# Routed expert layer: tokens sorted by expert in DRAM quarter by quarter, and the matmuls of 17 full slots placed around the convolution of the last quarter

## The chip, the cores and the metric

One Trainium2 chip (trn2), one core. The metric is the device time of one execution in microseconds (µs). The kernel before has a median of 687.84 µs over three runs (686.28, 688.94, 687.84).

## The reference, cut to what matters

The input has 8 sequences of 512 tokens with 1024 channels in float32, which are 4096 tokens in all. A depthwise causal convolution with 8 taps runs over each sequence, a router picks one of 8 experts for each convolved token, the token is multiplied by that expert's 1024 x 1024 matrix, and the original `x` is added.

```python
y = conv_general_dilated(x, cond_2048[:, None, :], window_strides=(1,), padding=[(7, 0)],
                         feature_group_count=1024) + L0_cond_b
idx = argmax(einsum('bsh,eh->bse', y, w_router), axis=-1)
all_out = einsum('bsh,efh->bsef', y, w_experts)
x = x + take_along_axis(all_out, idx[:, :, None, None], axis=2)[:, :, 0, :]
```

The inputs come from a fixed seed. For experts 0 to 7 the router's choices add up to 128, 227, 851, 1092, 528, 741, 367 and 162 tokens. In the first three quarters of the tokens they add up to 90, 173, 630, 839, 407, 527, 283 and 123.

## The kernel before, in words

The 1024 channels are 8 chunks (`HC`) of 128 partitions, and the 4096 tokens are four groups (a quarter each: two sequences, eight tiles of 128 tokens).

**Convolution.** For each group and chunk `x_sb` holds the channels as partitions and the tokens as columns. Of the 64 chunk-taps of a group TensorE takes 18, as matmuls by diagonal matrices (`conv()`, L525, two instructions for each of the two sequences), ScalarE takes one tap or the copy out of PSUM together with the bias (`seed()`, L277 and L282), and VectorE takes 42 as multiply-adds over 1024 columns (L359). TensorE then turns each finished chunk by transposes (`turn_y()`, L547) and interleaves the router's matmuls with them (`logits_of()`, L532). ScalarE copies the turned pieces out (`copy_out()`, L292), and SyncE stores them as rows of tokens in `y_dram` (`store_y()`).

**Routing, once, for all 32 tiles.** VectorE picks the expert of each token (L390 to L396), TensorE counts by two matmuls (L583, L584), and VectorE places each token (L402 to L422). One-hot matrices on VectorE and GpSimd and 32 small matmuls (L594) give the token of each row of each slot. A slot is 128 rows of one expert; each expert has its tokens rounded up to whole slots, 35 in all here.

**Slots.** Two slots are in flight (`RING`). For each slot GpSimd looks its indices up (L667), gathers 128 rows of `y_dram` (L682) and of `x` (L692), TensorE turns the rows back to channels by 8 transposes (`turn()`, L604), ScalarE writes the high part of a float32r pair (L323) and VectorE the rest (L478). TensorE does 48 matmuls of 512 columns (`gemm()`, L626: high by high, high by low, low by high), VectorE adds `x` (`residual()`, L472), and GpSimd scatters the 128 rows to `out` (L700). Where a slot begins another expert, ScalarE (`high()`, L298) and VectorE (`low()`, L365) split that expert's 8 weight chunks from `w_raw` into `w_sb`, each chunk once the slot ahead is through with it; SyncE refills `w_raw` behind them. There are seven such changes of expert.

TensorE alternates, by this order in `block.tensor`:

```python
turn(i, 1, False)
gemm(i, 0, False)
with pe.If(i < full):
    turn(i + 1, 0, False)
    gemm(i, 1, False)
```

## Time and profile before

| | |
|---|---|
| median of three runs | 687.84 µs (686.28 to 688.94) |
| the profiled execution: its time, its span | 687.4 µs, 685.6 µs |
| mean granted TensorE clock | 0.957 |
| TensorE (PE) busy | 635.6 µs, 93% |
| VectorE (DVE) busy | 382.0 µs, 56% |
| ScalarE (ACT) busy | 174.2 µs, 25% |
| GpSimd (POOL) busy | 157.1 µs, 23% |
| DMA | 118.13 MB, mean 172 GB/s |

The span runs from the first to the last instruction of the core. PE stands for TensorE's matmuls, PEld for its weight loads, POOLq and SPq for the queues on which GpSimd and SyncE issue DMAs. The granted clock is a share of 2.4 GHz: 1.00 is 2.4 GHz and 0.50 is 1.2 GHz. Matmul ends are modelled, so the spacing of many matmuls says more than the length of one.

### The profile page before, as it was taken

How to read it: one execution, taken by the hardware profiler on the slowest of the kernel's cores; microseconds unless marked ns; L12 is line 12 of the kernel's file. 1: busy time of each engine (PE TensorE's matmuls, PEld its weight loads, DVE VectorE, ACT ScalarE, POOL GpSimd, SP SyncE). 2: the span in 40 equal slices, each digit the busy share in tenths (PEclk: the TensorE clock that was granted, in tenths of full speed). 3: DMA queues.
4: the chain of work that ended last, by engine and by line, in shares of the span. 5: the costliest groups of instructions: out<-in, count | busy, mean ns of one | idle time of the engine just before them, and what ended most of it. 6: DMA issues, size and time to landing. Idle time of an engine off the chain costs nothing.

```text
span 685.6 us, 9583 instructions
## 1 busy us (share of the span) xinstructions
PE 635.6 (93%) x3058; PEld 488.1 (71%) x3059; DVE 382.0 (56%) x345; ACT 174.2 (25%) x199; POOL 157.1 (23%) x206
## 2 busy tenths in 40 slices
PE   1999999999999449999999999999999999999991
PEld 0556566666758338888888888888888888888881
DVE  5699999999999867531217212124411712181710
ACT  2124243323415215510106000014201500060600
POOL 5700000000000140233223332222323332222421
PEclk9989999999997559999999999999999999999996
DMA  8735275275321669574436743344743843476310
GB/s 291 290 124 161 84 246 165 86 238 182 107 78 62 214 206 371 195 287 148 142 122 218 258 144 124 126 135 148 294 144 104 317 156 127 128 277 220 96 65 8
DMA packets 50844, 118.13 MB, mean 172 GB/s; under 512 B 5520, under 2 KB 22032, under 8 KB 50832
## 3 DMA queue, kind: packets, MB, share of 16 engines
q1 hardware_dynamic: 35280, 67.64, 28.2%
q0 software_dynamic: 15552, 50.34, 21.9%
q8 instruction: 6, 0.10, 0.1%
q14 instruction: 6, 0.05, 0.0%
HBM read 89.13 MB, written 35.13 MB: 181 GB/s over the span
## 4 chain that ended last, share of the span: by engine, by line
PE 72%; issue 13%; DVE 9%; DMA 1%; POOL 1%; ACT 1%; SPq 0%; DVEq 0%; POOLq 0%; ACTq 0%
PE ps L626 56%; PE ps L525 8%; DVE y_t L359 6%; PE ps L604 5%; PE ps L547 2%; PE ps L532 1%; POOL diag L653 1%; DMA cst<-consts 1%; DVE x_sb L431 1%; DMA rows<-y_dram,idx 1%; DVE x_sb L428 0%; ACT y_t L277 0%; DVE x_sb L424 0%; DVE ys L478 0%; DVE rows L472 0%
## 5 line engine op out<-in xcount | busy, mean ns | idle before, releaser
L626 PE MATMUL ps<-w_sb,ys 128*128 128x512 f32 x1680 | 395.2, 394 | 0.0
L626 PEld LDWEIGHTS ps<-w_sb,ys 128*128 128x128 f32 x1680 | 314.1, 189 | 67.1
L359 DVE SCALAR_TENSOR_TENSOR y_t<-x_sb,taps,y_t 128x1024 f32<-128x1024 f32 x168 | 203.5, 1288 | 13.6 <-ACT y_t L282 7.0
L478 DVE TENSOR_TENSOR ys<-ps,ys 128x1024 fp32r<-128x1024 f32 x36 | 44.1, 1224 | 260.4 <-ACT ys L323 260.0
L525 PE MATMUL ps<-x_sb,diag 128*128 128x512 f32 x288 | 131.9, 613 | 13.9 <-POOL diag L653 13.9
L323 ACT CAST ys<-ps 128x1024 fp32r<-128x1024 f32 x36 | 36.5, 1014 | 317.6 <-PE ps L604 317.6
L525 PEld LDWEIGHTS ps<-x_sb,diag 128*128 128x128 f32 x288 | 55.1, 196 | 78.4 <-issue 78.4
L532 PEld LDWEIGHTS ps<-wr,y_t 128*128 128x128 f32 x512 | 76.4, 217 | 6.1 <-issue 4.3
L365 DVE TENSOR_TENSOR w_sb<-w_raw,w_sb 128x1024 fp32r<-128x1024 f32 x64 | 76.0, 1222 | 5.2 <-ACT w_sb L298 1.6
L532 PE MATMUL ps<-wr,y_t 128*128 128x8 f32 x512 | 75.6, 229 | 1.6 <-DVE y_t L359 1.6
L547 PE MATMUL ps<-cst,y_t 128*128 128x128 f32 x256 | 71.3, 316 | 0.8 <-ACT rows L292 0.8
L298 ACT CAST w_sb<-w_raw 128x1024 fp32r<-128x1024 f32 x64 | 66.5, 1050 | 19.4 <-PE ps L626 19.4
L700 POOL DMA_INDIRECT out<-rows,idx x35 | 36.2, 1034 | 118.1 <-DVE rows L472 101.0
L547 PEld LDWEIGHTS ps<-cst,y_t 128*128 128x128 f32 x256 | 54.6, 217 | 5.8 <-issue 4.2
L277 ACT ACTIVATE y_t<-ps,bias 128x1024 f32<-128x1024 f32 x16 | 17.9, 1116 | 127.1 <-PE ps L525 127.1
L662 POOL TENSOR_TENSOR x_sb<-x_sb,cst 128x1312 bf16<-128x1312 f32 x1 | 2.4, 2379 | 202.8 <-DVE x_sb L424 202.8
L604 PE MATMUL ps<-cst,rows 128*128 128x128 f32 x288 | 39.1, 281 | 9.8 <-DMA rows<-y_dram,idx 7.2
L667 POOL COPY idx<-ids_i 128x1 int32 (+1 forms) x73 | 18.1, 248 | 128.1 <-DMA out<-rows,idx 119.0
L472 DVE TENSOR_TENSOR rows<-ps,rows 128x1024 f32<-128x1024 f32 x35 | 42.5, 1216 | 7.6 <-PE ps L626 7.6
L692 POOL DMA_INDIRECT rows<-x_rows,idx x36 | 39.7, 1103 | 29.7 <-POOL idx L667 28.1
L682 POOL DMA_INDIRECT rows<-y_dram,idx x37 | 38.8, 1048 | 30.4 <-POOL idx L667 30.4
L604 PEld LDWEIGHTS ps<-cst,rows 128*128 128x128 f32 x288 | 34.9, 145 | 14.7 <-issue 7.4
(58 smaller groups left out, 107.5 us busy)
## 6 DMA issues: line engine op xcount, KB each, us to landing
w_raw<-experts SPq DMA_DIRECT2D x64, 512.0 KB, 6.0
x_sb<-x_t SPq DMA_DIRECT2D x32, 512.0 KB, 4.9
y_dram<-rows SPq DMA_DIRECT2D x16, 1024.0 KB, 5.6
rows<-y_dram,idx POOLq DMA_INDIRECT x37, 4.9
rows<-x_rows,idx POOLq DMA_INDIRECT x36, 4.4
out<-rows,idx POOLq DMA_INDIRECT x35, 3.4
cst<-consts SPq DMA_DIRECT2D x1, 377.0 KB, 9.1
cst<-consts SPq DMA_DIRECT2D x1, 64.0 KB, 5.1
```

The source lines that it names most:

```text
L298: nc.scalar.copy(w_sb[:, c * H:(c + 1) * H], w_raw[:, c % RAW, :]).then_inc(w_hi, 1)
L359: nc.vector.scalar_tensor_tensor(out=y, in0=x_sb[:, c, :, k:k + SEQ], scalar=taps[:, c, k:k + 1], in1=y, op0=ALU.mult, op1=ALU.add).then_i ...
L365: nc.vector.tensor_tensor(w_sb[:, (HC + c) * H:(HC + c + 1) * H], w_raw[:, c % RAW, :], w_sb[:, c * H:(c + 1) * H].bitcast(F32), ALU.subtr ...
L472: nc.vector.tensor_tensor(x_row[:, k, :], out_ps[k], x_row[:, k, :], ALU.add).then_inc(res_done, 1)
L478: nc.vector.tensor_tensor(ys[:, LO, k, :, :].rearrange("p c s -> p (c s)"), turn_both, ys[:, HI, k, :, :].rearrange("p c s -> p (c s)").bi ...
L525: mm = nc.tensor.matmul(conv_ps[n % 2][:, b, :], diag[:, DIAG[c, k], :], x_sb[:, c, b, k:k + SEQ], start=(k == PE_TAPS[c][0]), stop=(k == ...
L532: return nc.tensor.matmul(ps[:, 4, bass.ds((g * TPG + j) * EXPERTS, EXPERTS)], y_t[:, c, :, :].rearrange("p b s -> p (b s)")[:, j * P:(j + ...
L547: tr = nc.tensor.transpose(turn_ps[h][:, q * P:(q + 1) * P], y_t[:, c, :, :].rearrange("p b s -> p (b s)")[:, j * P:(j + 1) * P], ident)
L604: tr = nc.tensor.transpose(turn_ps[c // 4][:, c % 4 * P:(c % 4 + 1) * P], y_row[:, k, c * P:(c + 1) * P], ident)
L626: mm = nc.tensor.matmul(out_ps[k][:, f * HALF:(f + 1) * HALF], ys[:, a, k, c, :], w_sb[:, (b * HC + c) * H + f * HALF:(b * HC + c) * H + ( ...
L682: nc.gpsimd.indirect_dma_start(y_row[:, k, :], None, y_dram, at, bounds_check=last_token, oob_is_err=False).then_inc(y_got[k], 16)
L692: nc.gpsimd.indirect_dma_start(x_row[:, k, :], None, x_rows, at, bounds_check=last_token, oob_is_err=False).then_inc(x_got[k], 16)
```

## The change

The whole kernel is rearranged. The tokens are in the order of the input still, and the arithmetic of each token is the same.

- **Routing by quarter.** `choose(g)`, `rank(g)` and `place_rows(g)` run for each quarter of 8 tiles, on VectorE, TensorE and VectorE, among the taps of the quarter behind it. Each expert owns a region of 4096 rows in DRAM, and a running `base` for each expert says how far it is filled.
- **Sorting on the way out.** TensorE turns 8 chunks of one tile at a time (`turn()`), ScalarE copies the rows of 128 tokens out, and GpSimd scatters them straight to their sorted rows in `y_sorted` (`scatter_y()`), and their token numbers to `id_sorted` (`scatter_ids()`). The stores to `y_dram`, the one-hot matrices, their matmuls and the gathers of `y` are gone.
- **Two waves.** After three quarters `first_table()` lists 17 full slots (`FIRST_WAVE`). Their matmuls start then. VectorE does 4 taps of the last quarter in the gap and 4 behind each of the next slots; TensorE does that quarter's router matmuls, turns and counts behind slots 3, 4, 7, 11, 12 and 13 (`BEHIND`). `second_table()` runs on VectorE ahead of slot 15 and lists the remaining 18 slots.
- **Expert order.** Wave one takes the fullest expert first, which is expert 3, and then the others in order: 3 (6 slots), 1 (1), 2 (4), 4 (3), 5 (3). Wave two goes on with expert 5 (3 slots), then 0 (1), 1 (1), 2 (3), 3 (3), 4 (2), 6 (3), 7 (2). A change of expert falls on slots 6, 7, 11, 14, 20, 21, 22, 25, 28, 30 and 33 (counted from 0), which are eleven instead of seven.
- **Slots turned by VectorE.** ScalarE's queue loads 128 sorted rows by four DMAs of 32 partitions (`load_y()`), so laid out that a 32 x 32 block transpose on VectorE (`turn_blocks()`) gives the channels as partitions. The `experts` input is permuted to match. The token numbers come by a fifth DMA (`load_idx()`).
- **Last quarter.** It has 46 taps on VectorE and 13 on TensorE.

```diff
-PE_COUNT = [0, 0, 5, 4, 0, 0, 5, 4]
+EARLY = 3
+FIRST_WAVE = -(-(EARLY * TPG * P - EXPERTS * (P - 1)) // P)
+PE_COUNT = [[0, 0, 5, 4, 0, 0, 5, 4]] * EARLY + [[0, 0, 5, 5, 3, 0, 0, 0]] * (GROUPS - EARLY)
...
+        GAP_TAPS = (3, 1)
+        SLOT_TAPS = 4
+        BEHIND = {3: [("logits", 0), ("logits", 1)], 4: [("logits", 2), ("logits", 3)], 7: [("logits", 4), ("logits", 5)],
+                  11: [("logits", 6), ("logits", 7), ("turn", 0), ("turn", 1)],
+                  12: [("rank", 0), ("turn", 2), ("turn", 3), ("turn", 4)], 13: [("turn", 5), ("turn", 6), ("turn", 7)]}
+        CHOOSE_AT, PLACE_AT, TABLE_AT, SCATTER_AT = 12, 13, 14, 13
...
+            def load_y(w, n):
+                row = row_of(w, n)
+                src = y_sorted.rearrange("(r p) n -> r p n", p=P)[bass.ds(row, 1)].rearrange(
+                    "r (t i) (q f) -> (r i) q t f", t=4, q=4)
+                for q in range(4):
+                    nc.scalar.dma_start(y_blk[32 * q:32 * q + 32, :, :, :].rearrange("p t m f -> p t (m f)"),
+                                        src[:, q]).then_inc(y_got, 16)
...
+            for t in range(FIRST_WAVE):
+                w1, n1 = entry(t + 1)
+                w2, n2 = entry(t + 2)
+                high_y(t + 1, (t + 1) % RING, t + 1 < RING)
+                if (w2, n2) == (1, 0):
+                    sorted_is_out(1)
+                load_y(w2, n2)
...
+                load_idx(w1, n1, (t + 1) % IDX_RING, (t + 1 - IDX_RING) // RING + 1 if t + 1 >= IDX_RING else None)
+                high_w(w1, n1, t + 1)
...
+            for g in range(EARLY):
+                if g == 0:
+                    add_taps(PER_GROUP[0])
+                    continue
+                add_taps(5)
+                choose(g - 1)
+                add_taps(7)
+                place_rows(g - 1)
+                if g == EARLY - 1:
+                    find_first()
+                add_taps(PER_GROUP[g] - 12)
+            add_taps(GAP_TAPS[0])
+            choose(EARLY - 1)
+            add_taps(GAP_TAPS[1])
+            place_rows(EARLY - 1)
+            first_table()
...
+            for c in range(HC):
+                low(0, c)
+            turn_blocks(0, True)
+            low_y(0, 0)
+            for t in range(FIRST_WAVE):
...
+                if t == TABLE_AT:
+                    second_table()
+                turn_blocks(t + 1, False)
+                if t:
+                    residual(t - 1, (t - 1) % RING, (t - 1) // RING + 1)
+                low_y(t + 1, k)
+                add_taps(SLOT_TAPS)
+                low_w(w1, n1)
...
-            def turn(i, k, first):
-                pe.wait_ge(y_got[k], (i + 1) * 16)
...
-                    tr = nc.tensor.transpose(turn_ps[c // 4][:, c % 4 * P:(c % 4 + 1) * P],
-                                             y_row[:, k, c * P:(c + 1) * P], ident)
...
+            for t in range(FIRST_WAVE):
+                gemm(t, t % RING, *entry(t), t == 0)
+                for what, j in BEHIND.get(t, ()):
```

**TensorE, one slot of the loop, before.** `slot_expert` is the table of experts; L604 are the transposes.

```order
L602 ISA
L604 MATMUL ps<-cst,rows 128x128 x8
L610 ISA
L610 TENSOR_LOAD slot_expert
L610 ISA x2
L615 REGISTER_ALU
L622 ISA
L626 MATMUL ps<-w_sb,ys 128x512 x12
```

**TensorE, the end of a slot of wave one and the start of the next, in the change.** `tab_i` is the table, L782 are the router's matmuls for one chunk of the last quarter.

```order
L858 REGISTER_ALU
L862 MATMUL ps<-w_sb,ys 128x512 x12
L782 MATMUL ps<-wr,y_odd 128x8 x16
L846 TENSOR_LOAD tab_i
L846 ISA x2
L858 ISA
```

The eight transposes between two slots are gone, and behind four of the 35 slots such router matmuls stand in their place.

**VectorE, one slot, before.**

```order
L477 REGISTER_ALU
L478 TENSOR_TENSOR ys<-ps,ys 128x1024
L470 ISA
L472 TENSOR_TENSOR rows<-ps,rows 128x1024
L488 ISA
L488 TENSOR_LOAD slot_first
```

**VectorE, one slot of wave one, in the change.** L670 turns the blocks, L502 are taps of the last quarter.

```order
L670 STREAM_TRANSPOSE y_cols<-y_blk 128x4x8x32
L684 TENSOR_TENSOR x_row<-ps,x_row 128x1024
L675 TENSOR_TENSOR ys<-y_cols,ys 128x1024
L502 SCALAR_TENSOR_TENSOR y_odd<-x_own,taps,y_odd 128x1024 x4
L687 TENSOR_LOAD tab_i
L687 ISA x2
```

The transpose stands ahead of both, and four taps stand ahead of the weights of the next expert.

**ScalarE, one slot of wave one, in the change.** Before, L323 stood alone in this place.

```order
L384 DMA y_blk<-y_sorted 32x4x256
L377 TENSOR_LOAD tab_i
L377 ISA x2
L392 ISA
L392 DMA idx<-id_sorted 128x1
L406 TENSOR_LOAD tab_i
```

The first row is the last of four like it. ScalarE now issues five DMAs between writing `ys` and the weights.

## Rows read from the trace of the kernel before

**Rows 1.** Busy time by stage: us; PE, PEld, DVE, ACT, POOL busy; granted clock; DMA.

```profile
14.00:218.00 204.00, 201.94 (x1008) 128.86 (x1008) 197.40 (x164) 71.07 (x94) 15.96 (x15) 0.97 0.47 159
218.00:254.50 36.50, 16.95 (x98) 14.36 (x99) 28.64 (x49) 5.52 (x9) 9.05 (x11) 0.55 0.54 180
254.50:671.20 416.70, 416.61 (x1954) 344.73 (x1952) 148.54 (x127) 93.65 (x91) 125.16 (x171) 1.00 0.52 180
```

**Rows 2.** The chain that ended last, by engine, share of the span.

```profile
PE 72%; issue 13%; DVE 9%; DMA 1%; POOL 1%; ACT 1%; SPq 0%; DVEq 0%; POOLq 0%; ACTq 0%
```

**Rows 3.** The same chain in order of time: start, us, what; slots.

```profile
254.88 12.42 PE ps L626 x48
...
422.57 11.00 PE ps L626 x48
433.57 0.87 PE ps L604 x8
434.44 11.00 PE ps L626 x48
```

**Rows 4.** VectorE's taps (L359) alone, from 34 to 214 us.

```profile
34.00:214.00 180.00, 179.15 (x150) 0.98 0.45 146
```

**Rows 5.** TensorE and ScalarE in the convolution: chain, timeline, timeline.

```profile
51.63 6.97 PE ps L525 x16
...
209.16 3.86 PE L532 MATMUL ps<-wr,y_t 128*128 128x8 f32 x34
...
223.60 0.59 ACT L292 COPY rows<-ps 128x512 f32<-128x512 f32 x1 [0.27 <-PE ps L547]
```

**Rows 6.** Timeline of VectorE in the routing.

```profile
222.26 0.42 DVE L391 TENSOR_REDUCE top<-logits 128x32 f32<-128x256 f32 x1
...
226.28 0.69 DVE L402 TENSOR_TENSOR_SCAN scan<-cst,ps 128x256 f32<-128x256 f32 x1 [1.55 <-PE ps L584]
...
227.91 0.17 DVE L408 TENSOR_SCALAR small<-small 128x8 f32<-128x8 f32 x1
228.12 0.17 DVE L410 TENSOR_TENSOR_SCAN small<-cst,small 128x8 f32<-128x8 f32 x1
```

**Rows 7.** Groups of the page: line, engine, operation, count; busy, mean ns; idle before.

```profile
L478 DVE TENSOR_TENSOR ys<-ps,ys 128x1024 fp32r<-128x1024 f32 x36 | 44.1, 1224 | 260.4 <-ACT ys L323 260.0
L323 ACT CAST ys<-ps 128x1024 fp32r<-128x1024 f32 x36 | 36.5, 1014 | 317.6 <-PE ps L604 317.6
L365 DVE TENSOR_TENSOR w_sb<-w_raw,w_sb 128x1024 fp32r<-128x1024 f32 x64 | 76.0, 1222 | 5.2 <-ACT w_sb L298 1.6
L298 ACT CAST w_sb<-w_raw 128x1024 fp32r<-128x1024 f32 x64 | 66.5, 1050 | 19.4 <-PE ps L626 19.4
L472 DVE TENSOR_TENSOR rows<-ps,rows 128x1024 f32<-128x1024 f32 x35 | 42.5, 1216 | 7.6 <-PE ps L626 7.6
L700 POOL DMA_INDIRECT out<-rows,idx x35 | 36.2, 1034 | 118.1 <-DVE rows L472 101.0
```

**Rows 8.** Three DMA lines: issue ns min/median/max (x, weights); landing us of gathered rows (L682).

```profile
L219 SPq DMA_DIRECT2D x_sb<-x_t x32: 542/555/1199, 1.2 to 167.8; - x32
...
L227 SPq DMA_DIRECT2D w_raw<-experts x64: 332/333/997, 9.2 to 614.2; - x64
...
DMA to landing us min/median/max: 2.2/4.9/7.8
```

**Rows 9.** Granted clock around the end of the convolution (columns as in Rows 1).

```profile
209.00:213.00 4.00, 4.00 (x38) 3.92 (x36) 4.00 (x4) 3.65 (x5) 0.00 (x0) 1.00 0.54 180
213.00:214.00 1.00, 0.01 (x1) 0.00 (x0) 1.00 (x2) 1.00 (x2) 0.00 (x0) 0.72 0.96 322
214.00:222.00 8.00, 7.40 (x34) 7.31 (x35) 7.66 (x8) 3.51 (x4) 0.00 (x0) 0.50 0.01 3
```

**Rows 10.** Timeline: VectorE's first work behind the last tap; slot 0's matmuls.

```profile
218.04 3.49 DVE L365 TENSOR_TENSOR w_sb<-w_raw,w_sb 128x1024 fp32r<-128x1024 f32 x3
...
254.53 12.77 PE L626 MATMUL ps<-w_sb,ys 128*128 128x512 f32 x48
```

More of the change, by code:

```diff
@@ L330, in slot @@
                     for c in range(HC):
                         act.wait_ge(gemm_chunk, (t - 1) * HC + c + 1)
[L333 to L341 removed]
+                        high(nth, c)
@@ L489, in slot @@
                 with dve.If(new == 1):
[L490 removed]
+                    nth_load = dve.value_load(tab_i[0:1, w, 1, bass.ds(n, 1)], min_val=1, max_val=2 * EXPERTS - 1)
                     for c in range(HC):
[L492 to L497 removed]
```

1066 lines of the change are left out of this document (625 added, 441 removed).

## The prediction

> **What bounds the kernel now.** I read the stages first [rows 1]. They show three stretches. Up to 218 µs VectorE is busy for 197 of 204 µs and TensorE nearly as long. From 218 to 254.5 µs hardly anything is full, and the granted clock is 0.55. From there to 671 µs TensorE is full and VectorE has 148.5 µs of work in 416.7 µs. The chain that ended last agrees: TensorE has 72% of it [rows 2]. In order of time a slot is 48 matmuls in 11.00 µs and 8 transposes in 0.87 µs, so 11.87 µs, 35 times [rows 3]. In the first stage 150 taps took 179.15 µs, 1.194 µs each [rows 4], so a quarter of 42 taps is 50.1 µs. The last tap ends at 218.0 µs and slot 0 starts at 254.5 µs, a gap of 36.5 µs [rows 10]. The change works on all three stretches: it shortens the first by a quarter, keeps the gap, and takes the transposes off TensorE; in return the last quarter and four more changes of expert have to fit into the slots.
>
> **Term A, when slot 0 starts.** VectorE has three quarters of taps: 218.0 - 50.1 = 167.9 µs. Among them now stand two times choose() and place_rows() (11 operations each) and the 9 of find_first(). Operations on 8 columns are 0.21 µs apart (227.91 to 228.12) [rows 6]; 31 x 0.21 = 6.5, so 174.4. Beside it TensorE has in a quarter 72 conv instructions at 6.97/16 = 0.436 (31.4 µs), 128 router instructions at 3.86/34 = 0.114 (14.5 µs) [rows 5] and 64 turns at 0.87/8 = 0.109 (7.0 µs) [rows 3]. The turns no longer alternate with router work, so they wait for ScalarE: two halves take 0.44 + 0.27 + 0.59 = 1.30 µs [rows 5] and not 0.87, which is 8 x 0.43 = 3.4 µs. With 1.2 for the counts that is 57.5 µs, against 52.4 µs on VectorE. TensorE falls behind by 5 µs in each of the second and third quarters, of which find_first() gives back 2 and the three taps in the gap 3.6 of their own time; I take 5 µs of waiting ahead of choose(2). From there it is a sum: 174.4 + 3.6 (three taps) + 5 = 183.0; choose() 1.3; the counts 2.3 (two matmuls were waited for 1.55 [rows 6], nine here, one tap inside); place_rows() 1.1; first_table() and what precedes it, 38 operations, 12 of them on 152 to 256 columns at 0.36 (between 0.21 and 0.46, for which 256 columns give 0.42 busy [rows 6]) and 26 at 0.21, 9.8; the eight low() of the first expert at 3.49/3 = 1.16 [rows 10], 9.3. Then VectorE's turn of slot 0 (1.2, below), ScalarE's high part 1.0 [rows 7], its four DMA issues at 0.55 [rows 8] and the last seed 1.1, together 5.5 µs, behind which TensorE may start. The sum is 212.3, with 0.7 for handing over 213 µs. **Term A is 213 - 254.5 = -41.5 µs.** The other branch, turned rows through eight scatters (1.03 each to issue [rows 7]), landings and the load of slot 0, ends near 205 by the same rows and is covered by the eight low(); without them it would set the start.
>
> **Term B, the transposes.** 35 x 0.87 = **-30.5 µs**, since TensorE sets the pace of every slot. The load of the table entry now follows matmuls without transposes between; I cost it at nothing: the kernel before has the same load between transposes and matmuls, and they follow each other without a gap (433.57 + 0.87 = 434.44 [rows 3]). At worst the 0.87 had hidden it and comes back.
>
> **Term C, the last quarter's work on TensorE behind slots.** 14.5 router, 7.0 turns, 1.2 counts and some 3.0 of waits for ScalarE's copies: **+25.7 µs**. The 26 conv instructions of chunk 3 and 4 stay in the gap, under VectorE's table.
>
> **Term D, VectorE too late.** No row shows its transpose of 1024 float32 columns. The nearest rows are one-pass operations of the same size at 1.22 [rows 7]; below, half of that, above, twice. I take 1.2. The Trainium skill (VectorE: DVE Perf Modes, The three transpose paths) lists 311 ns for 128 columns of bf16; scaled by its own formula for the fixed part that is an estimate of about 1.25 µs, and no run here shows it. An iteration of wave one is then 3 x 1.22 + 4 x 1.19 = 8.4 µs and fits under 11.0. With a change of expert it is 8.4 + 8 x 1.2 = 18.0. Slots 6 and 7 change both: 36.0 against two slots and one slot of lead, 33.0, costs 3.0. The second table, 46 operations (11 long), is 11.5 µs. It stands behind the weights of slot 14, which end 2.3 µs into that slot (1.05 and 1.22 behind its predecessor's last chunk [rows 7]), and ahead of the turn, the residual and the low part of slot 15: 2.3 + 11.5 + 3.7 = 17.5 against 11.0 costs 6.5. In wave two ScalarE issues five DMAs, 2.8 µs, ahead of the first weights, so VectorE waits 2.4 and an iteration with a change is 3.7 + 2.4 + 9.6 = 15.7. Slots 20, 21 and 22 are 47.1 against 33.0 and a lead of 8: 6.1. Slots 28 and 30 lose 2.0. **Term D is +17.6 µs.** GpSimd loses the look-ups and one of three indirect DMAs per slot and is never last; SyncE's queue loses the stores, and its weights are asked for earlier.
>
> **Term E, the clock.** Slot 0 took 12.42 and not 11.00 µs behind the idle gap [rows 3]. I count four more such falls behind the waits above: **+5.6 µs**.
>
> **Sum.** -41.5 - 30.5 + 25.7 + 17.6 + 5.6 = -23.1, against the profiled execution's own 687.4 µs: **664.3 µs**. That execution lies 0.4 µs below the median of 687.84, so the two are the same here. The tail behind the last slot stays.
>
> **The rivals.**
> - *The ring of the y loads.* There is one `y_blk`. Each slot needs VectorE's turn 1.2, ScalarE's high part 1.0, four issues 2.2, and the landing L, one after the other: 4.4 + L. Above L = 6.6 µs this replaces 11.0 as the pace, and from there each change of expert costs its 4.7 in full, as no lead is left. Rows gathered from `y_dram` landed in 4.9 µs in the middle and 7.8 at most [rows 8]. For: four times 128 KB beside weights, with ScalarE issuing in the midst. Against: the median. At L = 7.0 it is 24 x 0.4 + 11 x 4.7 - 11.1 already counted = +50, less some 8 where term C overlaps: 706. It is the case of the other sign. Chance 0.13.
> - *TensorE slow in the first stage.* The granted clock fell to 0.50 behind a pause of 1.3 µs at 213 µs and stayed there for 8 µs, although TensorE was busy for 7.40 of them with router matmuls [rows 9]. Such stretches now stand in every quarter. The Trainium skill (TensorE: Matmul & The Clock Gate, Part 1) says that a sustained busy stretch releases the throttle; by it this rival would cost nothing, and the row speaks against relying on it. If half of the 21.5 µs of turns and router work and 3 µs of conv per quarter run at 0.50, two quarters lose 2 x (10.8 + 3) = 28, of which VectorE's slack covers some 12: 680. Chance 0.14.
> - *VectorE's transpose takes two passes.* 2.3 instead of 1.2 µs: 11 x 1.1 on the changes of expert and 8 of lead, +20: 684. Chance 0.10, split evenly between no change and slower.
> - *It goes better than I count.* Issues at 0.33 as for the weights [rows 8], no lag of TensorE, no falls of the clock: -5 - 6 - 4 = 649. Chance 0.15.
> - That it would not do what it says (the slots not starting before the last quarter) is excluded by the order of TensorE, which has slot 0 ahead of that quarter's router work.
>
> **How the numbers follow.** The forecast has 0.48, its own range 655 to 676. What a measurement can tell from no change is 0.5%, so 684.4 to 691.3. Faster: 0.48 + 0.14 + 0.15 = 0.77; same 0.05; slower 0.13 + 0.05 = 0.18. The range goes from the good case, 647, to where the ring has just begun to decide, 702.
>
> **What would show it.** First matmul of the slots at 213 µs (a later one: term A, and the wait ahead of choose(2) tells whether TensorE was behind). Slots without late work 11.0 µs apart (more: the ring, with VectorE waiting for `y_blk`). The transpose at 1.2 µs busy. Long slots at 3, 4, 7, 11 to 13 (term C), at 7, 15, 21 and 22 (term D). The prediction is wrong if the plain slots aren't near 11.0 or if slot 0 starts behind 225 µs.

## The result, and the profile after

The changed kernel took 754.52 µs (median of four executions, 742.73 to 755.06) against 687.06 for the kernel before beside it: a ratio of 1.087, 95% interval 1.076 to 1.098. Slower, where 664.3 was forecast, and 52 µs beyond the range. A second series gave 750.65 (six executions, 746.94 to 759.4, ratio 1.092, interval 1.088 to 1.097); single edits below are held against that one. The profiled execution is the shortest of all, 742.73 µs with a span of 740.9. The executions of 754 µs and more show a little less clock (0.89 to 0.90 against 0.91) and are not explained further than that, nor is one execution of e15 below, which took 938.09 µs at a mean clock of 0.64.

The page of the changed kernel: busy time, clock, DMA, and the engines' shares of the chain that ended last (TensorE had 72% there [rows 2]).

```profile
span 740.9 us, 9397 instructions
PE 640.8 (86%) x2752; PEld 483.2 (65%) x2753; DVE 476.8 (64%) x518; ACT 203.3 (27%) x231; POOL 202.6 (27%) x172
...
PEclk9997988799798599999999998699988999998997
...
DMA packets 67076, 139.90 MB, mean 189 GB/s; under 512 B 14304, under 2 KB 33760, under 8 KB 67040
...
PE 50%; DMA 14%; issue 10%; ACTq 8%; DVE 6%; ACT 6%; POOL 4%; DVEq 0%; SPq 0%; POOLq 0%
```

The same core by stretches (start and end, length, busy time and instructions of each engine, granted clock, DMA share, GB/s): the convolution up to the third `choose()`, the gap, slots 0 to 14, the crossing from one table to the other, and slots 17 to 34.

```profile
core 0: us, PE busy (x) PEld busy (x) DVE busy (x) ACT busy (x) POOL busy (x), PEclk, DMA share, GB/s
14.00:203.50 189.50, 186.14 (x767) 116.97 (x768) 156.71 (x156) 53.11 (x65) 62.06 (x52) 0.88 0.54 130
203.50:255.20 51.70, 23.81 (x107) 13.96 (x106) 24.23 (x62) 11.97 (x19) 19.22 (x16) 0.76 0.69 181
255.20:459.90 204.70, 194.67 (x922) 161.50 (x922) 153.11 (x176) 59.35 (x66) 54.06 (x44) 0.96 0.63 199
459.90:498.90 39.00, 27.84 (x96) 21.67 (x96) 7.16 (x6) 2.09 (x2) 12.17 (x13) 0.80 0.77 218
498.90:729.10 230.20, 208.09 (x864) 168.87 (x864) 128.06 (x110) 72.76 (x74) 46.99 (x38) 0.94 0.71 227
```

Held against [rows 1] and the forecast: slot 0 starts at 255.2, not at 213 (+42). Slots 0 to 14 with the last quarter behind them take 204.7 as against some 203 by the slots themselves with term C and the part of term D that falls there (+2). Slots 15 and 16 take 39.0, where two slots are 22 (+17). Slots 17 to 34 take 230.2; 18 slots at 11.0 and the forecast's 8 to 10 for changes of expert make 208 (+22). The tail gives 3 back. These make 80; the difference between 664.3 and 742.7 is 78, so they cover it within the rounding of the forecast's parts.

Where VectorE waited, from its timeline (start, length, engine, line, operation; in brackets the idle time ahead and what ended it):

```profile
139.83 0.23 DVE L527 TENSOR_REDUCE top<-ps 128x8 f32<-128x64 f32 x1 [9.94 <-PE ps L782]
203.54 0.22 DVE L527 TENSOR_REDUCE top<-ps 128x8 f32<-128x64 f32 x1 [8.01 <-PE ps L782]
218.57 9.17 DVE L660 TENSOR_TENSOR w_sb<-w_raw,w_sb 128x1024 fp32r<-128x1024 f32 x8
250.17 1.25 DVE L670 STREAM_TRANSPOSE y_cols<-y_blk 128x1024 f32<-128x1024 f32 x1 [22.43 <-DMA y_blk<-y_sorted]
...
301.64 1.22 DVE L684 TENSOR_TENSOR x_row<-ps,x_row 128x1024 f32<-128x1024 f32 x1 [2.58 <-PE ps L862]
...
475.29 1.25 DVE L670 STREAM_TRANSPOSE y_cols<-y_blk 128x1024 f32<-128x1024 f32 x1 [15.53 <-DMA y_blk<-y_sorted]
495.11 1.25 DVE L670 STREAM_TRANSPOSE y_cols<-y_blk 128x1024 f32<-128x1024 f32 x1 [16.25 <-DMA y_blk<-y_sorted]
...
530.90 9.17 DVE L660 TENSOR_TENSOR w_sb<-w_raw,w_sb 128x1024 fp32r<-128x1024 f32 x8 [5.30 <-ACT w_sb L368]
548.84 9.18 DVE L660 TENSOR_TENSOR w_sb<-w_raw,w_sb 128x1024 fp32r<-128x1024 f32 x8 [5.19 <-ACT w_sb L368]
```

The second and third `choose()` waited 9.9 and 8.0 µs for the router's matmuls (L782): TensorE, not VectorE, was last in the convolution. The eight `low()` ended at 227.7, and then VectorE waited 22.4 µs for the rows of slot 0. Plain slots are 10.9 µs apart, waiting for matmuls (L862), as forecast. The turns of slots 16 and 17, which follow the second table, waited 15.5 and 16.3 µs for rows. And at a change of expert VectorE waits over 5 µs for ScalarE's first high part (L368); the first three changes of the second wave, which follow each other directly, are 17.9 µs apart, where 15.7 was forecast.

TensorE ahead of the second and third `choose()`, where the router's matmuls of four chunks stand in one run of 64 instructions (L782), and the convolution's instructions (L768) behind the first and second such run:

```profile
73.21 8.72 PE L768 MATMUL ps<-x_own,diag 128*128 128x512 f32 x16
...
130.12 9.66 PE L782 MATMUL ps<-wr,y_odd 128*128 128x8 f32 x64
139.64 9.64 PE L768 MATMUL ps<-x_own,diag 128*128 128x512 f32 x16
...
192.75 10.75 PE L782 MATMUL ps<-wr,y_even 128*128 128x8 f32 x64
```

64 router instructions take 9.7 to 10.8 µs, where 64 times the 0.114 µs of [rows 5] is 7.3, and 16 conv instructions take 8.7 to 9.6 behind them instead of 6.97 [rows 5].

### The profile page after: what moved, and what is told of

Same layout as the page of the kernel before. It is cut to its first block, busy times and chain, and to the rows that moved or that the text cites. A ratio compares the mean times of both kernels' runs of the same rounds, so it can differ in the third digit from the quotient of the medians.

```text
span 740.9 us, 9397 instructions
## 1 busy us (share of the span) xinstructions
PE 640.8 (86%) x2752; PEld 483.2 (65%) x2753; DVE 476.8 (64%) x518; ACT 203.3 (27%) x231; POOL 202.6 (27%) x172
## 4 chain that ended last, share of the span: by engine, by line
PE 50%; DMA 14%; issue 10%; ACTq 8%; DVE 6%; ACT 6%; POOL 4%; DVEq 0%; SPq 0%; POOLq 0%
PE ps L862 23%; PE ps L768 16%; DMA y_blk<-y_sorted 9%; PE ps L782 9%; ACTq L384 4%; ACT w_sb L368 4%; DVE y_cols L670 3%; PE ps L804 3%; DVE w_sb L660 2%; DMA y_sorted<-row_own,fill_i 2%; ACTq L377 2%; POOL y_sorted L911 1%; POOL id_sorted L922 1%; DMA idx<-id_sorted 1%; POOL y_sorted L931 1%
## 5 line engine op out<-in xcount | busy, mean ns | idle before, releaser
L862 PE MATMUL ps<-w_sb,ys 128*128 128x512 f32 x1680 | 407.2, 405 | 66.8 <-ACT y_odd L342 26.8
L862 PEld LDWEIGHTS ps<-w_sb,ys 128*128 128x128 f32 x1680 | 329.3, 197 | 143.5 <-DVE w_sb L660 27.8
L670 DVE STREAM_TRANSPOSE y_cols<-y_blk 128x1024 f32<-128x1024 f32 x36 | 44.7, 1241 | 123.2 <-DMA y_blk<-y_sorted 123.2
L942 POOL DMA_INDIRECT x_row<-x_rows,idx x36 | 43.1, 1198 | 253.5 <-DMA idx<-id_sorted 212.3
L368 ACT CAST w_sb<-w_raw 128x1024 fp32r<-128x1024 f32 x96 | 93.4, 1045 | 60.1 <-PE ps L862 32.1
L502 DVE SCALAR_TENSOR_TENSOR y_odd<-x_own,taps,y_odd 128x1024 f32<-128x1024 f32 x74 | 90.8, 1279 | 4.8 <-ACT y_odd L346 4.6
L768 PE MATMUL ps<-x_own,diag 128*128 128x512 f32 x160 | 79.7, 658 | 13.8 <-POOL diag L897 13.8
L502 DVE SCALAR_TENSOR_TENSOR y_even<-x_own,taps,y_even 128x1024 f32<-128x1024 f32 x56 | 70.3, 1303 | 15.7 <-ACT y_even L346 6.9
L950 POOL DMA_INDIRECT out<-x_row,idx x35 | 45.0, 1286 | 121.1 <-DVE x_row L684 115.8
L768 PEld LDWEIGHTS ps<-x_own,diag 128*128 128x128 f32 x160 | 33.4, 214 | 53.6 <-issue 53.6
L684 DVE TENSOR_TENSOR x_row<-ps,x_row 128x1024 f32<-128x1024 f32 x35 | 41.7, 1191 | 22.4 <-PE ps L862 22.4
L768 PE MATMUL ps<-x_ext,diag 128*128 128x512 f32 x108 | 52.5, 641 | 0.0
L675 DVE TENSOR_TENSOR ys<-y_cols,ys 128x1024 fp32r<-128x1024 f32 x36 | 44.1, 1226 | 6.2 <-ACT ys L401 4.5
L922 POOL DMA_INDIRECT id_sorted<-token,pos_i x32 | 41.7, 1304 | 9.8 <-issue 9.8
L782 PEld LDWEIGHTS ps<-wr,y_even 128*128 128x128 f32 x256 | 36.4, 229 | 2.9 <-issue 2.4
L768 PEld LDWEIGHTS ps<-x_ext,diag 128*128 128x128 f32 x108 | 21.6, 206 | 25.5 <-issue 25.5
L782 PE MATMUL ps<-wr,y_even 128*128 128x8 f32 x256 | 35.8, 282 | 0.0
L502 DVE SCALAR_TENSOR_TENSOR y_even<-x_ext,taps,y_even 128x1024 f32<-128x1024 f32 x28 | 34.8, 1278 | 0.1
L782 PEld LDWEIGHTS ps<-wr,y_odd 128*128 128x128 f32 x256 | 33.2, 211 | 1.8 <-issue 1.4
```

Of the source, the lines that this page charges most:

```text
L368: nc.scalar.copy(w_sb[:, c * H:(c + 1) * H], w_raw[:, c, :]).then_inc(w_hi, 1)
L502: nc.vector.scalar_tensor_tensor(out=y, in0=x_tile(g, c)[:, :, k:k + SEQ], scalar=taps[:, c, k:k + 1], in1=y, op0=ALU.mult, op1=ALU.add).t ...
L670: nc.vector.transpose(y_cols[:, :, :].rearrange("p m (t i) -> p t m i", t=4), y_blk[:, :, :, :]).then_inc(y_blocks, 1)
L675: nc.vector.tensor_tensor(ys[:, LO, k, :, :].rearrange("p c s -> p (c s)"), y_cols[:, :, :].rearrange("p c s -> p (c s)"), ys[:, HI, k, :, ...
L684: nc.vector.tensor_tensor(x_row[:, k, :], out_ps[k], x_row[:, k, :], ALU.add).then_inc(res_done, 1)
L768: mm = nc.tensor.matmul(conv_ps[n % 2][:, b, :], diag[:, DIAG[c, k], :], x_tile(g, c)[:, b, k:k + SEQ], start=(k == 0), stop=(k == PE_COUN ...
```

## The experiments

Four causes were on the table. **Theory 1**: the 32 scatters of 4-byte ids clog the DMA engines. **Theory 2**: TensorE's clock falls behind the long router runs and makes it last in the convolution. **Theory 3**: the 4 MB of the second expert's weights, asked for at 220 µs, hold up the rows of slot 0. **Theory 4**: what ScalarE issues ahead of the first high part stretches a change of expert. Each was first edited without the others; e1 leaves out the eight late fills too, the scatters by which GpSimd pads each expert's last block of 128 rows.

| run | edit | µs | ratio to before (95%) |
|---|---|---|---|
| e11 | none, the changed kernel again | 750.65 | 1.0922 (1.0879 to 1.0965) |
| e1 | no id scatters, no late fills | 729.89 | 1.0604 (1.0547 to 1.0662) |
| e2 | second expert's weights behind slot 0's rows | 741.43 | 1.0777 (1.0751 to 1.0803) |
| e3 | one conv unit moved within the router's run | 752.6 | 1.0954 (1.0889 to 1.1019) |
| e4 | ids asked for by GpSimd | 737.6 | 1.0716 (1.0689 to 1.0743) |
| e5 | router matmuls between conv matmuls | 738.87 | 1.0753 (1.0711 to 1.0795) |
| e6 | two conv taps fewer on TensorE | 740.71 | 1.0754 (1.0694 to 1.0813) |
| e7 | second table behind the slot's work | 751.39 | 1.0947 (1.0897 to 1.0996) |
| e16 | ids of 32 bytes | 728.07 | 1.0568 (1.0537 to 1.0598) |
| e13 | two row buffers | 724.96 | 1.0541 (1.0516 to 1.0566) |
| e14 | turns back in the second wave | 754.07 | 1.0967 (1.0924 to 1.101) |
| e8 | e4 and ids in the rows | 711.63 | 1.0378 (1.0319 to 1.0438) |
| e10 | e9 with id scatters | 721.49 | 1.0495 (1.0465 to 1.0525) |
| e9 | all mends | 687.44 | 1.0004 (0.9982 to 1.0026) |
| e12 | e9 and two row buffers | 672.95 | 0.9768 (0.9743 to 0.9794) |
| e15 | e12, turns back in the second wave | 683.93 | 0.9926 (0.9904 to 0.9949) |

### Theory 1: scatters of 4 bytes (e1, e8, e16)

```diff
 for g in range(EARLY):
     scatter_y(g)
-    scatter_ids(g)
+# id_sorted is written once at the start from a constant list (e1)
```

> The 32 scatters of 4-byte token ids and the 8 late scatters that fill the last blocks are left out. The ids come from a constant table (a fixed list of all tokens, with the real number per expert), written to id_sorted at the start; the rest rows are copied there at the start too, so the later gathers, scatters and loads move as many bytes as before. The rows that leave are therefore paired with other tokens' x. Theory 1 (these tiny transfers clog the DMA engines and hold up the loads of sorted rows): the last tap of the third quarter moves from 191.9 to about 187, slot 0 starts at 245 instead of 255.2 (landing of its rows 7 us instead of 13.8), the two waits of 15.5 and 16.3 us at slots 16 and 17 shrink to under 3 us together with the second table's, total about 716 against 742.7. Rival (weights asked for at the same moment, theory 3, and ScalarE's issues, theory 4, hold the rows up): slot 0 at 253, wait at slot 16 still 10 us, total 735.

e1 pairs rows with the wrong tokens' `x`, so it is no version of the layer and only its time counts. It took 729.89, 21 µs less than the changed kernel. The rows of slot 0 were there 36.0 µs behind the third `choose()` instead of 46.6, as theory 1 had it, and the residual of slot 16 came 65 µs behind that of slot 12, not 81. The start of the slots gained less than that, since this execution's third `choose()` came at 210.4, with a 12.6 µs wait for TensorE. But the forecast of 716 was missed, and 735 was the rival's: slots 16 and 17 still waited 9.4 and 8.6 µs for rows, not under 3. So the scatters (with the fills) cost 21 µs here, and of the waits that remain, 11.0 µs at slot 0 and these two, they are not the cause.

e8 keeps the result whole and carries the id in the row:

```diff
-y_sorted = nc.dram_tensor("y_sorted", [EXPERTS * TOKENS, H], F32, ...)
+y_sorted = nc.dram_tensor("y_sorted", [EXPERTS * TOKENS, H + 8], F32, ...)
+nc.gpsimd.tensor_copy(row_buf(g, j)[0][:, H:].bitcast(I32), token[:, n:n + 1].to_broadcast([P, 8]))
```

> The token's id travels in eight added columns of each sorted row (1032 columns), written by GpSimd ahead of the scatter; the 32 scatters of 4-byte ids are gone, and nothing of the result changes. It has the ids loaded by GpSimd as in the run before, so it is held against that run's 737.6 us. Theory 1 (4-byte scatters clog the DMA engines): rows of slot 0 land 8 to 10 us earlier behind the third choose, residual of slot 14 to that of slot 17 falls from 76 us to 62, total 714. Rival (bytes and issues, not their size): within 5 us of 737.6, or above it, since rows of 4128 bytes are more bytes and GpSimd has 32 copies more.

711.63 against e4's 737.6: 26 µs, as theory 1 has it. VectorE's wait for slot 0 fell to 12.3, slot 16's residual came 66 µs behind slot 12's instead of e4's 76 (the expectations of e7 and e8 name slots 14 and 17 for this stretch, but their 81 and 76 are the times from slot 12 to 16), and from `choose()` to the rows it is 36.3 µs:

```profile
203.34 0.23 DVE L507 TENSOR_REDUCE top<-ps 128x8 f32<-128x64 f32 x1 [8.39 <-PE ps L762]
...
239.61 1.25 DVE L650 STREAM_TRANSPOSE y_cols<-y_blk 128x1024 f32<-128x1024 f32 x1 [12.26 <-DMA y_blk<-y_sorted]
```

e16 asks what about the scatters does it, with as many of them and elements of 32 bytes:

```diff
-id_sorted = nc.dram_tensor("id_sorted", [EXPERTS * TOKENS, 1], I32, ...)
+id_sorted = nc.dram_tensor("id_sorted", [EXPERTS * TOKENS, 8], I32, ...)
```

> The changed kernel with every id repeated eight times in its sorted row, so that the 32 id scatters move elements of 32 bytes instead of 4, as many of them as before; the initial fill of the id table is 1 MB instead of 128 KB. If the element's size of 4 bytes is what clogs the DMA engines, most of theory 1's gain comes without carrying the ids in the rows: rows of slot 0 land 36 to 38 us behind the third choose instead of 46.6, residual of slot 12 to that of slot 16 falls from 81 to 66 us, total 725 to 730. If the number of tiny elements does it (128 per scatter, whatever their size), everything stays: 745 to 755.

728.07: as much as e1 gained. The rows came 36.9 µs behind `choose()`, slot 16's residual 71 µs behind slot 12's. So between these two it is the size of 4 bytes and not the number of elements; sizes between 4 and 32 bytes were not tried. ScalarE asked for the rows of slot 0 at the same time in both, at 230.6 and 231.6 µs, but its four issues took 9.0 µs in the changed kernel and 1.9 in e16. At the crossing e16 parts the two waits. Slot 16's falls from 15.5 to 2.6 µs, slot 17's does not:

```profile
457.26 1.25 DVE L670 STREAM_TRANSPOSE y_cols<-y_blk 128x1024 f32<-128x1024 f32 x1 [2.61 <-DMA y_blk<-y_sorted]
482.06 1.25 DVE L670 STREAM_TRANSPOSE y_cols<-y_blk 128x1024 f32<-128x1024 f32 x1 [21.16 <-DMA y_blk<-y_sorted]
```

The DMA view of one stretch, 116 to 136 µs, in which SyncE loads `x` for the next quarter: first the changed kernel, then e16. Both issue the eight id scatters of the first quarter from about 101 to 115 µs; their last 32 packets are recorded inside the stretch in the changed kernel and ahead of it in e16. In these views q0 is GpSimd's queue, q1 SyncE's and q10 ScalarE's.

```profile
DMA packets 554, 1.02 MB, mean 51 GB/s; under 512 B 55, under 2 KB 55, under 8 KB 554
...
q1 hardware_dynamic: 522, 1.02, 90.2%
q0 software_dynamic: 32, 0.00, 0.1%
...
x_ext<-x_t SPq DMA_DIRECT2D x2, 512.0 KB, 17.8
```

```profile
DMA packets 1089, 2.11 MB, mean 106 GB/s; under 512 B 64, under 2 KB 64, under 8 KB 1088
...
q1 hardware_dynamic: 1088, 2.10, 33.1%
...
x_ext<-x_t SPq DMA_DIRECT2D x3, 512.0 KB, 3.6
```

The id packets themselves are 32 in 20 µs and take 0.1% of the engines' time, so a list by queue clears them. The harm is in the other queue: 522 packets of 2 KB hold the engines for 90% of 16 x 20 µs, 0.55 µs each, while e16's take 0.10, and a load of 512 KB lands in 17.8 µs instead of 3.6. It is the same from 451 to 461 µs, where both kernels issue id scatters and ScalarE's queue (q10) brings the rows of slot 16. In the changed kernel 10 of its packets hold 45% of 16 x 10 µs, in e16 720 hold 17%:

```profile
q10 hardware_dynamic: 10, 0.01, 45.2%
```

```profile
q10 hardware_dynamic: 720, 0.53, 17.3%
```

What inside an engine holds these packets up, no trace shows.

### Theory 3 and theory 4 (e2, e4)

```diff
 sp.wait_ge(table_ready, w + 1)
+if w == 0:
+    sp.wait_ge(y_got, 64)
```

> SyncE asks for the second expert's weights only when the rows of slot 0 have landed. Theory 3 (the 4 MB burst holds those rows up): their last landing falls from 13.8 us to 7, slot 0 starts at 248 and the total is 736. Theory 1 (the id scatters do): landing stays at 11 to 13 us, slot 0 at 253, total 741. Either way slot 3 or so may wait for weights by up to 3 us if the delay is too long.

741.43, 9 µs less by the medians, though its profile ends level with the changed kernel's shortest execution. The wait for slot 0's rows fell from 22.4 to 13.7, so the burst does hold them up; but slot 1's then waited 9.8 behind it, and of the 8 µs it was ahead at slot 3 it had lost 3 by slot 6, where the first changes of expert wait for these weights. The burst was moved more than removed. Theories 1 and 3 share these rows: the burst and the scatters are in flight together, and what each takes alone can't be added.

```diff
-load_idx(1, n + 1, r, ...)            # ScalarE
+load_idx(1, n + 3, (m + 3) % IDX_RING)  # GpSimd, a slot ahead
```

> The 36 loads of a slot's ids leave ScalarE's queue and are issued by GpSimd, one slot ahead. Theory 4 (in the second wave ScalarE's issues and table reads ahead of the first high part make a change of expert 18.0 us): VectorE's wait for it falls from 4.9 to 3.2 us, consecutive changes stand 16.3 apart, some 9 changes give 12 us, total 731. Rival (it is DMA traffic): changes stay 17.5 to 18.0 apart, total 741 to 745, and the later issues on GpSimd's queue cost up to 5.

737.6. The wait for ScalarE's first high part fell from over 5 µs to about 3, and the changes stand 15.9 and 15.6 µs apart, which is what the prediction had counted, though with five issues on ScalarE, where four are left here:

```profile
531.58 9.17 DVE L644 TENSOR_TENSOR w_sb<-w_raw,w_sb 128x1024 fp32r<-128x1024 f32 x8 [2.64 <-ACT w_sb L368]
...
547.45 9.18 DVE L644 TENSOR_TENSOR w_sb<-w_raw,w_sb 128x1024 fp32r<-128x1024 f32 x8 [3.10 <-ACT w_sb L368]
...
563.09 8.04 DVE L644 TENSOR_TENSOR w_sb<-w_raw,w_sb 128x1024 fp32r<-128x1024 f32 x7 [2.90 <-ACT w_sb L368]
```

Theory 4 stands. Of the queue's order `load_y()`, `load_idx()`, `high_w()`, the one small load with its table read was worth 2.1 µs per change. The 731 expected was set against the short execution of 742.7; against 750.65 the gain is the 12 to 13 µs forecast.

### Theory 2: TensorE in the convolution (e3, e5, e6)

```diff
-conv(g + 1, 2)
 for c in range(4, 6):
     logits(g, c)
+conv(g + 1, 2)
```

> In every quarter the conv of chunk 2 of the next quarter stands between the router work of chunks 4, 5 and that of 6, 7, so that no 32 router matmuls follow each other. Theory 2 (TensorE's granted clock falls behind the long run of router matmuls and makes TensorE the bound of the convolution): granted clock at 0.50 only for half as long between 60 and 200 us, the wait ahead of the third choose falls from 8.0 to 3 us, slot 0 starts at 250, total 737. Rival (the fall comes from router matmuls in any grouping, or TensorE is simply too full): waits unchanged within 1.5 us, total 742 to 745, as the conv that VectorE needs comes later.

752.6: nothing gained. But the edit does not do what its expectation says. Each chunk is 16 router instructions. In the changed kernel they stand in runs of 32, 32 and 64, and moving the conv behind chunks 4 and 5 makes runs of 32, 64 and 32: the run of 64 is moved, not cut. TensorE's timeline in the first quarter, from chunks 2 and 3 on, has the 64 parted only by a wait of 1.75 µs for VectorE:

```profile
50.40 3.63 PE L782 MATMUL ps<-wr,y_even 128*128 128x8 f32 x32
55.78 7.00 PE L782 MATMUL ps<-wr,y_even 128*128 128x8 f32 x32 [1.75 <-DVE y_even L502]
62.63 10.45 PE L768 MATMUL ps<-x_own,diag 128*128 128x512 f32 x20
72.92 3.89 PE L782 MATMUL ps<-wr,y_even 128*128 128x8 f32 x32
76.66 8.54 PE L768 MATMUL ps<-x_own,diag 128*128 128x512 f32 x16
```

Behind the 64 router instructions 20 conv instructions took 10.45 µs, where 20 x 0.436 is 8.7, and behind the 32 the 16 took 8.54, where 6.97 is their time at full clock. The mean clock from 73 to 139.8 µs is 0.82, where the changed kernel has 0.83. So e3 says nothing for or against shorter runs. e5 spreads the router matmuls, some four to eight instructions behind every two of the convolution:

```diff
-for c in range(2): logits(g, c)
-conv(g, 7)
-for c in range(2, 4): logits(g, c)
-conv(g + 1, 2)
-for c in range(4, 6): logits(g, c)
+mixed([conv_parts(g, 7)], [logit_parts(g, c) for c in (0, 1)])
+mixed([conv_parts(g + 1, 2)], [logit_parts(g, c) for c in range(2, 6)])
```

> The router matmuls of chunks 0 to 5 stand one by one between the conv matmuls of chunk 7 and of the next quarter's chunk 2 (two or three behind each), so that at most 32 router instructions follow each other, as in the kernel before. Theory 2a (long runs of 8-column matmuls make the granted clock fall): mean clock of 73 to 203 us 0.95 instead of 0.85, third choose at 196 instead of 203.5, slot 0 at 248, total 736. Theory 2b (the clock falls in the turns, with their waits for ScalarE's copies, or by itself): clock and choose as before within 2 us, total 740 to 745.

738.87, 12 µs less. Between 73 and 139.8 µs the granted clock is 0.97, where the changed kernel had 0.83 with as busy a TensorE (64.45 and 65.29 of 66.80 µs). In the kernel before, whose clock was 1.00 there, the router's matmuls stand two instructions at a time between transposes. The same stretch of the changed kernel, of e5 and of the kernel before:

```profile
73.00:139.80 66.80, 65.29 (x276) 41.56 (x277) 52.77 (x53) 17.50 (x24) 23.94 (x16) 0.83 0.59 126
```

```profile
73.00:139.80 66.80, 64.45 (x317) 40.12 (x316) 63.39 (x74) 20.65 (x29) 24.77 (x17) 0.97 0.50 126
```

```profile
73.00:139.80 66.80, 66.80 (x380) 44.74 (x379) 66.23 (x56) 25.85 (x36) 0.00 (x0) 1.00 0.43 140
```

The third `choose()` comes at 187.2 instead of 203.5, 4 µs from the forecast's 183.0. Theory 2 stands, with fine interleaving as the cure. It is not a full one: e5 keeps a run of 32 in each quarter, and behind it 16 conv instructions still take 8.8 µs and not 6.97. Whether it is the 8 columns of these matmuls or something else about them, no run shows. Against the changed kernel's profile only 5 µs of the 16 were left at the last slot's residual (724 against 729); the rest was taken back on the way (e5 was 16 µs ahead at slot 6 and 9 at slot 17).

```diff
-PE_COUNT = [[0, 0, 5, 4, 0, 0, 5, 4]] * EARLY + ...
+PE_COUNT = [[0, 0, 5, 3, 0, 0, 5, 3]] * EARLY + ...
```

> In the first three quarters chunks 3 and 7 have three taps on TensorE instead of four; VectorE has 44 taps a quarter instead of 42. Theory 2 (TensorE is the bound of the convolution): it has 3.5 us a quarter less at full clock, VectorE's waits ahead of the chooses (1.8, 9.9, 8.0 us) shrink to 0 to 3, the third choose comes at 195 to 197, slot 0 at 248, total 736. Rival (VectorE sets the pace and its waits are only phase): the last tap comes 7 us later, third choose at 207 to 210, total 748.

740.71, and the third `choose()` at 192.4: more work for VectorE, less for TensorE, 11 µs earlier. TensorE was the bound of the convolution.

### The crossing between the tables (e7)

```diff
-if t == TABLE_AT: second_table()
 turn_blocks(t + 1, False)
 ...
 low_y(t + 1, k)
+if t == TABLE_AT: second_table()
```

> VectorE makes the second table behind the turn, the residual and the low part of slot 15 instead of ahead of them, and the rest rows may be filled as soon as their numbers are known, some 10 us ahead of the table's end. If the 12.9 us table is what sets slots 15 to 17 apart: the rows of slots 16 and 17 are asked for 10 us earlier, residual of slot 14 to that of slot 17 falls from 81 us to 66, total 728. Theory 1 (the DMA engines are clogged by id scatters and fills at just that time): the rows of slot 16 and 17 still take 15 us to land, gain under 6 us, total 737 to 740.

751.39: a miss, no gain. The slots up to 14 gained, but everything was given back at one place: slot 17's turn waited 30.1 µs. GpSimd had issued its eighth fill at 479.6, behind eight id scatters, and ScalarE could ask for the rows only at 499.2.

```profile
479.59 0.97 POOL L933 DMA_INDIRECT y_sorted<-row_own,fill_i  x1 [0.30 <-issue]
499.17 1.77 ACTq L385 DMA_DIRECT2D y_blk<-y_sorted  x4
503.46 1.25 DVE L672 STREAM_TRANSPOSE y_cols<-y_blk 128x1024 f32<-128x1024 f32 x1 [30.09 <-DMA y_blk<-y_sorted]
```

The table was late, and behind it the fills were later still. In the same stretch SyncE's eight weight loads, 4 MB asked for from 471.3 µs on, fill the DMA engines at some 410 GB/s. What the id scatters and what the weights take of these 20 µs was not tested. In the other kernels it is the same gate: e8 still waits 11.3 µs there.

### All mends, and the scatters again (e9, e10)

e9 takes e8, e5 and e7, puts the third quarter's turns ahead of the last conv units, writes ids one tile ahead, and does the last quarter two slots earlier:

```diff
-SLOT_TAPS = 4
-CHOOSE_AT, PLACE_AT, TABLE_AT, SCATTER_AT = 12, 13, 14, 13
+SLOT_TAPS = 5
+CHOOSE_AT, PLACE_AT, TABLE_AT, SCATTER_AT = 10, 11, 12, 11
```

> All mends together, the result unchanged: ids in the rows (written one tile ahead), ids of a slot loaded by GpSimd, router matmuls between conv matmuls, the turns of the third quarter ahead of the last conv units, the last quarter's taps five per slot instead of four so that its look-up stands two slots earlier, the second table behind the slot's own work, the rest rows filled as soon as they are known. If the ledger is right the parts add: 711.6 less 14 (third choose at 188 instead of 203.3), less 4 (turns and ids), less 18 (slots 14 to 17 in 48 us instead of 66): 676, faster than the kernel before (687.3). Rival: what is taken from one wait goes to the next (the clock, the rows' landing of 6 us behind each turn, VectorE's 15.7 us at changes of expert, which now come close behind each other): 695 or more.

> The same mends, but the ids in scatters of 4 bytes as in the changed kernel. Theory 1: slot 0 10 to 12 us later than in the run above (the branch of the rows is now the only one), at the late scatters 5 to 15 us more, unless the two slots of slack hide them: 690 to 700. Rival (the 4-byte scatters cost only where nothing else hides them, and the slack hides both): within 4 us of the run above.

> The changed kernel once more, nothing edited, to know which time the single edits are held against: four executions gave 742.7, 754.2, 754.9 and 755.1. If the granted clock behind the router runs is the difference (theory 2), the times fall in two groups again, some 12 us apart, and the long ones show the first choose at 80 us and the third at 210, not at 73 and 203.5. Rival: they fall anywhere between.

e9 took 687.44: 24 µs less than e8, not the 36 hoped for, and level with the kernel before. e10, the same with 4-byte ids, took 721.49. So the scatters cost 34 µs here, more than alone, and more than the 690 to 700 expected for e10 allow. That with everything else earlier the rows are the last thing is a reading and was not tested.

```profile
189.70 0.22 DVE L508 TENSOR_REDUCE top<-ps 128x8 f32<-128x64 f32 x1 [5.12 <-PE ps L810]
...
225.37 1.25 DVE L652 STREAM_TRANSPOSE y_cols<-y_blk 128x1024 f32<-128x1024 f32 x1 [10.78 <-DMA y_blk<-y_sorted]
```

```profile
187.70 0.22 DVE L512 TENSOR_REDUCE top<-ps 128x8 f32<-128x64 f32 x1 [3.09 <-PE ps L814]
...
239.91 1.25 DVE L656 STREAM_TRANSPOSE y_cols<-y_blk 128x1024 f32<-128x1024 f32 x1 [25.83 <-DMA y_blk<-y_sorted]
```

From `choose()` to the rows it is 35.7 µs in e9 and 52.2 in e10. The second half is at the crossing: slot 16's residual behind slot 10's by 79 and 93 µs. e11 shows no two groups of times, so its expectation failed: its profiled execution took 749.2 with the third `choose()` at 202.7, as in the short one. Both kinds of start do occur: the profiles of e1 and e7, with the same convolution, have the first `choose()` at 80 and the third at 210. But 6 µs of the spread are there without it, and what they come from stays open.

### One row buffer, and what the transposes were worth (e12 to e15)

Slots 17 to 34 were still slow. There is one `y_blk`, and its next load can be asked for only behind the turn and the high part.

```diff
+y_next = over("y_next", [P, 4, HC, PIECE], diag_at)
-high_y(t + 1, ...)
-load_y(1, n + 2)
+load_y(1, n + 2, (FIRST_WAVE + k) % 2, t + 1)
+high_y(t + 1, ...)
```

> As the run with all mends, and a second buffer for the loaded rows (y_next, over the conv diagonals, free by then), so that ScalarE issues the four loads of slot t+2 ahead of the high part of slot t+1 instead of behind it. If in the second wave VectorE's chain sets the pace (a change of expert 15.6 us, the iterations behind it 7 to 9 us of which 3.6 to 8.7 us wait for rows), the waits for rows vanish, the change costs 14 as ScalarE's first high part comes 1.8 us earlier, and TensorE sets the pace again: from slot 17 on 18 slots in 205 us instead of 229, total 663. Rival (landing and DMA traffic, so that two loads in flight take twice as long): 220 us and 680.

> The second row buffer alone, on the changed kernel (751 us by its ten executions so far). Second wave 205 to 212 us instead of 230 (a change of expert 16.2 instead of 18.0, no waits for rows), waits around slots 15 to 17 unchanged, total 730. Rival (in the changed kernel the waits for rows are only phase behind the changes of expert of 18 us): 745.

Alone it is worth 26 µs, where 21 were expected, by the medians the largest of the single edits (e16 has 23, and their intervals overlap). The crossing is no shorter: instead of the waits of 15.5 and 16.3 µs at slots 16 and 17 there is one of 34.2 at slot 17. From the residual of slot 16 to that of slot 34: 223 µs in the changed kernel, 203 in e13, 214 in e9, 203 in e12. The second wave of e12:

```profile
456.00:659.00 203.00, 198.95 (x864) 162.57 (x863) 127.98 (x110) 76.03 (x74) 58.81 (x56) 0.99 0.77 250
...
508.27 2.36 DVE L650 TENSOR_TENSOR w_sb<-w_raw,w_sb 128x1024 fp32r<-128x1024 f32 x2 [0.42 <-ACT w_sb L368]
...
533.04 1.25 DVE L660 STREAM_TRANSPOSE y_cols<-y_blk 128x1024 f32<-128x1024 f32 x1 [9.83 <-DMA y_blk<-y_sorted]
```

TensorE is busy for 199 of 203 µs at 0.99, where it had 208 of 230 at 0.94. The waits for ScalarE at a change are 0.3 to 1.3 µs. The waits for rows did not vanish as expected: 8 to 10 µs are left behind changes of expert, where ScalarE issues the next rows only behind its last high part (518.2 behind 517.3 µs); now a slot of lead covers them. At 672.95, 2.3% under the kernel before, this is the first version that beats it. It missed its 663 by 10, since the second wave gave 12 µs and not 24; 5 more came ahead of it (profiled executions of 690.41 and 673.28). e12 against e9 is the second buffer alone; e9 itself joins several edits, and what each gives there was measured only for the ids (e10).

```diff
+if w == 1:
+    for c in range(HC):
+        nc.tensor.transpose(turn_ps[c // 4][:, ...], ys[:, HI, k, c, :].bitcast(F32), ident)
```

> Eight TensorE transposes of the slot's rows, whose result nobody reads, ahead of each slot's matmuls in the second wave only: the work that the change took off TensorE. If TensorE sets the pace there, 18 slots by 0.87 us cost 15.7: 767. If VectorE's chain sets it (the theory), only slots that TensorE bounds pay: 3 to 7 us, 754 to 758.

> The same eight transposes per slot of the second wave, on the kernel with all mends and two row buffers. There TensorE should be the bound again, so they cost 12 to 16 us against that kernel's own time. If they cost under 7, VectorE's chain still sets the pace there.

On the changed kernel the 18 x 8 transposes cost 3 µs (754.07 against 750.65, intervals overlap), on e12 11.0 µs (683.93 against 672.95). The work is the same in both, 15.7 µs by 18 x 0.87. So in the second wave of the changed kernel, where VectorE's chain sets the pace, TensorE's transposes are nearly free, and taking them away brought nearly nothing; in e12 they cost 11, a little under the 12 to 16 expected.

## Why the prediction was wrong, point by point

**Term A failed, by 42 µs in two halves.** First, "I take 5 µs of waiting ahead of choose(2)", hence 183.0: it was 203.5. The turns took what was counted (about 1.3 per tile), while from 139.6 µs to the third `choose()` conv was busy for 36.2 µs, not 31.4, and the router's matmuls for 18.0, not 14.5, for the clock. This was the second rival, named with a chance of 0.14 and priced at 680; e5 puts `choose()` at 187.2 once the clock holds. From 73 to 139.8 µs TensorE was busy for 65.29 of 66.80 µs at a mean clock of 0.83, as it was busy at 0.50 in [rows 9]. The Trainium skill (TensorE: Matmul & The Clock Gate, Part 1) says that a sustained busy stretch releases the throttle; the trace does not agree. Second, the other branch, the rows' way to slot 0, "ends near 205 by the same rows and is covered by the eight low()". It ended at 250. The forecast gives no sum for the 205, that is 22 µs from `choose()` to the rows, and 46.6 were measured. The last row scatter was issued until 222.9 µs, ScalarE could ask for the rows at 230.6, its four issues took 9.0 µs where 2.2 were counted, and the rows were there at 250.2. 36 to 37 of the 46.6 µs are there without the 4-byte scatters (e1, e8, e9, e16), longer than VectorE's 24.2 of table and low parts. The step allowed for the issues and the landings of [rows 8], and nothing for scatters, weights and loads sharing the engines: the 4-byte scatters account for some 10 µs, and the weight burst for some 8 (e2: 38.4 µs from `choose()` to the rows), two parts that can't be added. The chain from `choose()` through the table to the last `low()` was counted right: 24.2 µs against 1.3 + 2.3 + 1.1 + 9.8 + 9.3 = 23.8.

**Term B was right per slot and wrong in place.** Plain slots are 10.9 µs apart, and the turn on VectorE takes 1.24 to 1.25 µs, near the 1.2 taken from the nearest rows. The estimate from the Trainium skill (VectorE: DVE Perf Modes, The three transpose paths) was 1.25, and the trace agrees. But "TensorE sets the pace of every slot" failed for the second wave: e14 shows some 3 of 15.7 µs there.

**Term C came right in the sum.** Slots 0 to 14 took 204.7 against 203, with the part of term D that falls there; the two were not measured apart.

**Term D failed, by 39 µs.** The second table was sized well (12.9 µs for 11.5). What was not counted is what is queued behind it: the fills wait for the table and for eight id scatters ahead of them on GpSimd, and slot 17's load waits for the fills. Slot 16's rows were held up by the 4-byte scatters (e16). The change of expert was 17.9 instead of 15.7: VectorE waited over 5 and not 2.4 µs for ScalarE's first high part. The five issues were counted, at 2.8 µs, the table read and the waits between them were not (e4, with four issues and no read for the ids, gives 15.6 to 15.9). And the ring of the y loads, the rival of the other sign, was right in its mechanism and wrong in its threshold. It said that the ring decides from a landing of 6.6 µs, since 4.4 + 6.6 = 11.0. That is the condition in a row of plain slots. In the second wave a plain iteration took 9.1 µs on average (of which turn, high part and issues are some 4.1, so about 5 is left for the landing), and one with a change 17.6: 11 x 9.1 + 7 x 17.6 = 223, as measured. So a plain one wins back 1.9 of the 6.6 that a change costs, and seven changes among 18 slots want more than that. e13 prices the single buffer at 26 µs, 20 of them in the second wave.

**Term E** was too small as well. The mean granted clock fell from 0.957 to 0.906. It was 0.88 instead of 0.97 in the convolution, and 0.94 to 0.96, with 0.80 at the crossing, in the slots, which had 1.00 before. The gap was not to blame (0.76, where it had 0.55). In slots 17 to 34 TensorE was busy for 208.1 µs, where 18 x 11.0 is 198, though there VectorE set the pace. What the falls cost in all was not tested.

**The unnamed cause** was the scatter of 4-byte elements, worth 21 to 34 µs (e1, e16, e8 against e4, e9 against e10). Nothing in the profile of before could price it: that kernel has no such scatter, and its smallest transfers were index loads. The prediction bounded the operation by its issue, 1.03 µs, and gave the landing no upper bound. Of that the range should have held something. (Its lower end, 647, is not quite its own good case either, which is 649.)
